# A state-space branch woven into six attention layers: which channels share a group, and how many groups one summing pass takes

## The reference, cut to what matters

```python
def step(hc, inp):                 # state-space branch, per channel d (256) and state n (16)
    a, b = inp
    hc = a * hc + b
    return (hc, hc)
...
A_disc = jnp.exp(delta[..., None] * A)
B_x = delta[..., None] * Bm[:, :, None, :] * x1[..., None]
...
y = jnp.einsum('tbdn,btn->btd', hs, Cm)      # a sum over the 16 states
out = (jax.nn.silu(g) * y) @ out_W + out_b
...
for i in range(DEPTH):             # second branch: six layers, windows of 32 tokens, 16 heads of 64
    x = attn_layer(shift_tokens(x), ...) + x
    x = ffn_layer(shift_tokens(x), ...) + x
...
x + s * silu(x_second)             # s is the first branch's result
```

## Time and profile before

| | us |
|---|---|
| median of three runs | 1931.85 |
| the profiled execution | 1930.3 |
| its span, first to last instruction | 1928.5 |
| TensorE busy in the span | 1756.7 |
| VectorE / GpSimd / ScalarE busy | 1596.1 / 1527.8 / 1252.5 |
| the 16 DMA engines, mean busy share | 32% |

### The profile page before, as it was taken

One profiled execution on the slowest core, in us unless ns is written; L12 is line 12 of the kernel. 1 busy time (PEld: TensorE's weight loads), 2 busy tenths in 40 slices (PEclk: granted clock), 3 DMA queues, 4 the chain that ended last, 5 costly groups with the idle time before them and its releaser, 6 DMA issues. The chain is left out here.

```text
span 1928.5 us, 73996 instructions
## 1 busy us (share of the span) xinstructions
PE 1756.7 (91%) x30944; PEld 999.4 (52%) x30944; DVE 1596.1 (83%) x2736; ACT 1252.5 (65%) x2339; POOL 1527.8 (79%) x1348
## 2 busy tenths in 40 slices
PE   3798999999999999999999999999999999999862
PEld 1355555555555555555555555555555555555420
DVE  5777998888888897889988898889878798888536
ACT  3566676676676676776776676676766666766630
POOL 1765899878998789878998789888888689987640
PEclk9999999999999999999999999999999999999975
DMA  3114234153313334142332433342331534123321
GB/s 109 29 39 70 45 71 79 37 85 49 66 33 67 72 61 71 41 71 55 68 71 37 87 49 59 74 79 39 67 58 33 100 62 63 30 45 58 54 23 44
DMA packets 95607, 113.14 MB, mean 59 GB/s; under 512 B 42334, under 2 KB 61548, under 8 KB 95276
## 3 DMA queue, kind: packets, MB, share of 16 engines
q1 hardware_dynamic: 95276, 108.41, 31.1%
HBM read 19.22 MB, written 1.05 MB: 11 GB/s over the span
## 5 line engine op out<-in xcount | busy, mean ns | idle before, releaser
L1315 POOL TENSOR_TENSOR AB<-qc,qn 128x512 f32<-128x512 f32 x384 | 494.6, 1298 | 21.4 <-DVE qn L1109 21.4
L1326 POOL TENSOR_TENSOR AB<-AB,rinv 128x512 f32<-128x512 f32 x384 | 402.0, 1062 | 24.5 <-DVE rinv L1132 24.5
L559 PE MATMUL bank<-wqkv,XT 128*128 128x512 f32 x768 | 400.2, 614 | 12.2 <-DVE qn L1109 12.2
L1333 POOL TENSOR_TENSOR Pb<-Pb,p_rden 128x512 f32<-128x512 f32 x192 | 200.1, 1042 | 235.2 <-DVE p_rden L1153 234.1
L848 ACT ACTIVATE qkT<-bank 128x512 f32<-128x512 f32 x384 | 229.2, 597 | 209.3 <-PE bank L584 208.6
L1109 DVE TENSOR_TENSOR qc<-bank,rt 128x512 f32<-128x512 f32 x384 | 261.3, 680 | 123.4 <-ACT sq L839 108.9
L584 PEld LDWEIGHTS bank<-ident,AB 128*128 128x128 f32 x1536 | 181.7, 142 | 181.9 <-issue 119.3
L839 ACT ACTIVATE sq<-bank 128x512 f32<-128x512 f32 x384 | 228.1, 594 | 66.4 <-PE bank L559 57.3
L1109 DVE TENSOR_TENSOR qn<-bank,rt 128x512 f32<-128x512 f32 x384 | 261.4, 681 | 0.0
L584 PE MATMUL bank<-ident,AB 128*128 128x128 f32 x1536 | 241.5, 280 | 13.3 <-ACT qkT L848 6.2
L1116 DVE TENSOR_REDUCE ssq<-sq 128x8 f32<-128x512 f32 x384 | 251.2, 670 | 0.0
(11 more groups left out here) (137 smaller groups left out, 2657.3 us busy)
## 6 DMA issues: line engine op xcount, KB each, us to landing
V<-V SPq DMA_DIRECT2D x672, 64.0 KB, 2.1
rep<-du SPq DMA_DIRECT2D x64, 512.0 KB, 7.3
wqkv<-in_Wqkv SPq DMA_DIRECT2D x36, 256.0 KB, 3.7
XV<-XT SPq DMA_DIRECT2D x96, 64.0 KB, 2.8
wo<-in_Wo SPq DMA_DIRECT2D x6, 512.0 KB, 4.1
BC<-BC SPq DMA_DIRECT2D x8, 256.0 KB
w<-in_W SPq DMA_DIRECT2D x6, 341.0 KB, 3.2
BC<-BC SPq DMA_DIRECT2D x8, 128.0 KB
```

What stands on the lines that cost most here:

```text
L559: pe.matmul(R[u % 2][:], XT[:, s % NB, (u % 2) * P:(u % 2 + 1) * P], wqkv[:, (u // 2) * 512:(u // 2 + 1) * 512], start=True, stop=True).th ...
L1315: pool.tensor_tensor(AB[:, n % NAB, :], qc[:, u % 2, :], qn[:, u % 2, :], ALU.add).then_inc(rs_done, 1)
L1326: pool.tensor_tensor(o, o, r, ALU.mult).then_inc(nm_done, 1)
L1333: pool.tensor_tensor(Pb[:, g % 2], Pb[:, g % 2], r, ALU.mult).then_inc(pn_done, 1)
```

## The change

Four things change, and the orders of all engines with them.

1. A transfer of `replicate` takes every eighth channel, `du[r::8]`, where it took 16 neighbours, `du[r:r + 16]`. The amount and the packets are the same. The rows of `A`, the columns of `in_W` and `in_b` that belong to the gate, and the rows of `out_W` are put into the matching order outside of the loop, when the inputs are laid out.
2. `ZSUM` is 4: `z_sum` takes 4 chunks, one for each strip, and there are 4 calls per batch. `chunk` numbers the chunks so that four in a row lie in four transfers and four strips; a transfer's two chunks are j and j + 4.
3. `NH` goes from 5 to 8 (`hb`), `NAB` from 12 to 9 (`AB`).
4. The lists of all engines are in another order, and some operations have another lag: `turn_p(i, 3)` and `value(i + 1, 1)`, `value(i + 1, 2)` end an iteration where they began the next; `norm_x` begins VectorE's odd iterations where it ended the even ones; the `z_` operations are spread over the phases in another way.

The hunks of ScalarE's and VectorE's lists are left out but for a few lines, and GpSimd's is cut to its last part.

```diff
@@ -38,24 +38,24 @@
 
 
 BSTEP = 6
-NAB = 12
+NAB = 9
 NREP = 4
-NH = 5
-ZSUM = 2
+NH = 8
+ZSUM = 4
 ROWS16 = (0, 2, 4, 6, 1, 3, 5, 7)
 BC_IN = 8 * 16
 V_IN = 7 * 16
 FIRST_TO_LAST = range(-2, STEPS + 9)
-T_ORDER = [("turn_p", 3, 1, 1), ("turn", 0, 0, 1), ("turn", 1, 0, 1), ("turn", 2, 0, 1), ("turn", 3, 0, 1),
-           ("turn_p", 0, 0, 1), ("turn", 4, 0, 1), ("turn", 5, 0, 1), ("turn_p", 1, 0, 1), ("turn", 6, 0, 1),
-           ("turn", 7, 0, 1), ("turn_p", 2, 0, 1)]
+T_ORDER = [("turn", 0, 0, 1), ("turn", 1, 0, 1), ("turn", 2, 0, 1), ("turn", 3, 0, 1), ("turn_p", 0, 0, 1),
+           ("turn", 4, 0, 1), ("turn", 5, 0, 1), ("turn_p", 1, 0, 1), ("turn", 6, 0, 1), ("turn", 7, 0, 1),
+           ("turn_p", 2, 0, 1), ("turn_p", 3, 0, 1)]
 X_ORDER = [("values_out", 3, 1, 1), ("scores", 0, 0, 1), ("scores", 1, 0, 1), ("values_out", 0, 0, 1),
            ("scores", 2, 0, 1), ("values_out", 1, 0, 1), ("scores", 3, 0, 1), ("values_out", 2, 0, 1)]
-M_ORDER = [("z_x", 0, -1, 6), ("z_dbc", 0, 1, 6), ("z_out", 0, 9, 6), ("z_g", 0, 5, 6), ("z_dup", 0, 1, 6),
-           ("z_decay", 13, 8, 6), ("z_decay", 1, 4, 6), ("z_decay", 6, 6, 6), ("z_decay", 2, 4, 6),
-           ("z_decay", 7, 6, 6), ("z_decay", 3, 5, 6), ("z_decay", 8, 7, 6), ("z_decay", 14, 8, 6),
-           ("z_decay", 9, 7, 6), ("z_decay", 10, 7, 6), ("z_decay", 4, 5, 6), ("z_decay", 15, 8, 6),
-           ("z_decay", 11, 7, 6), ("z_decay", 12, 7, 6), ("z_decay", 0, 3, 6), ("z_decay", 5, 5, 6)]
+M_ORDER = [("z_dbc", 0, 1, 6), ("z_out", 0, 9, 6), ("z_dup", 0, 1, 6), ("z_x", 0, -2, 6), ("z_g", 0, 4, 6),
+           ("z_decay", 8, 6, 6), ("z_decay", 14, 8, 6), ("z_decay", 9, 6, 6), ("z_decay", 0, 3, 6),
+           ("z_decay", 15, 8, 6), ("z_decay", 5, 5, 6), ("z_decay", 3, 4, 6), ("z_decay", 11, 7, 6),
+           ("z_decay", 1, 3, 6), ("z_decay", 4, 4, 6), ("z_decay", 12, 7, 6), ("z_decay", 10, 6, 6),
+           ("z_decay", 6, 5, 6), ("z_decay", 13, 7, 6), ("z_decay", 7, 5, 6), ("z_decay", 2, 3, 6)]
 
 
 def befores(order):
@@ -374,8 +374,8 @@
 
         def chunk(j):
 
-            n = 2 * (j // 4) + j % 2
-            return n, ROWS16[n], (j // 2) % 2
+            n = 4 * (j // 8) + j % 4
+            return n, ROWS16[n], (j // 4) % 2
 
         def xpair(s):
             b = s % NB
@@ -493,39 +493,39 @@
                 sp.wait_ge(delta_done, b + 1)
                 k = 8 * b + n - NREP
                 if k >= 0:
-                    chunks = 16 * (k // 8) + 4 * (k % 8 // 2) + 3 + k % 2
+                    chunks = 16 * (k // 8) + 8 * (k % 8 // 4) + 5 + k % 4
                     sp.wait_ge(dA_done, chunks)
                     sp.wait_ge(bu_done, chunks)
-                r = 16 * ROWS16[n]
+                r = ROWS16[n]
                 sp.dma_start(rep[:, (8 * b + n) % NREP].rearrange("p z c t -> p (z c t)"),
-                             du[r:r + 16].rearrange("d (o z) c t -> d o (z c t)", o=1).broadcast_to([16, 8, 2 * DBLK * SEQ]))\
+                             du[r::8].rearrange("d (o z) c t -> d o (z c t)", o=1).broadcast_to([16, 8, 2 * DBLK * SEQ]))\
                   .then_inc(rep_in[(8 * b + n) % NREP], 16)
 
             for i in FIRST_TO_LAST:
-                replicate(i - 4, 2)
-                next_qk(i, 1)
-                replicate(i - 7, 5)
                 replicate_bc(i - 3, 0)
-                replicate(i - 6, 4)
-                replicate_bc(i - 4, 4)
-                replicate(i - 3, 0)
+                replicate_bc(i - 3, 1)
+                next_qk(i, 2)
+                spread(i, 0)
                 next_v(i, 0)
+                replicate_bc(i - 3, 2)
+                replicate(i - 5, 4)
+                replicate_bc(i - 3, 3)
+                replicate_bc(i - 3, 4)
+                next_qk(i, 3)
+                replicate(i - 6, 6)
                 arrange_x(i + 2)
-                replicate(i - 7, 6)
-                replicate(i - 7, 7)
-                replicate_bc(i - 3, 1)
-                replicate_bc(i - 3, 2)
-                spread(i, 0)
-                next_qk(i, 2)
-                replicate(i - 5, 3)
-                replicate(i - 3, 1)
                 spread(i, 1)
-                next_qk(i, 3)
+                replicate(i - 5, 5)
+                spread(i, 2)
+                spread(i, 3)
                 next_v(i, 1)
-                spread(i, 2)
+                replicate(i - 6, 7)
                 next_qk(i + 1, 0)
-                replicate_bc(i - 3, 3)
-                spread(i, 3)
+                replicate(i - 3, 2)
+                replicate(i - 3, 3)
+                replicate(i - 2, 0)
+                next_qk(i + 1, 1)
+                replicate(i - 2, 1)
                 other_weights(i)
 
         @block.tensor
@@ -760,64 +760,60 @@
             pe.wait_ge(pool_set, POOL_SET)
             pe.wait_ge(mask_set, 2)
             for i in FIRST_TO_LAST:
-                z_x(i + 1)
-                turn_p(i - 1, 3)
-                value(i, 1)
-                value(i, 2)
+                z_dbc(i - 1)
                 turn(i, 0)
                 values_out(i - 1, 3)
+                turn(i, 1)
                 value(i, 3)
-                turn(i, 1)
-                qk(i + 1, 0)
-                qk(i + 1, 1)
                 scores(i, 0)
                 turn(i, 2)
-                z_sum(i - 5, 0)
+                z_out(i - 9)
+                qk(i + 1, 0)
+                z_dup(i - 1)
+                z_x(i + 2)
                 w_out(i - 2, 0)
-                z_dbc(i - 1)
                 turn(i, 3)
-                z_out(i - 9)
-                z_g(i - 5)
+                qk(i + 1, 1)
+                scores(i, 1)
+                turn_p(i, 0)
                 qk(i + 1, 2)
-                z_dup(i - 1)
-                scores(i, 1)
+                z_g(i - 4)
+                w_gelu(i - 3, 0)
+                turn(i, 4)
+                w_out(i - 2, 1)
+                values_out(i, 0)
                 qk(i + 1, 3)
-                w_out(i - 2, 1)
-                turn_p(i, 0)
-                w_gelu(i - 3, 0)
+                w_gelu(i - 3, 1)
                 qk(i + 1, 4)
-                turn(i, 4)
-                values_out(i, 0)
-                w_gelu(i - 3, 1)
+                w_out(i - 2, 2)
                 turn(i, 5)
+                w_gelu(i - 3, 2)
                 qk(i + 1, 5)
-                w_out(i - 2, 2)
-                w_gelu(i - 3, 2)
                 scores(i, 2)
                 turn_p(i, 1)
+                w_gate(i - 3, 0)
                 qk(i + 1, 6)
-                w_gate(i - 3, 0)
                 w_out(i - 2, 3)
                 turn(i, 6)
                 values_out(i, 1)
-                z_sum(i - 8, 6)
                 w_gate(i - 3, 1)
                 turn(i, 7)
-                z_sum(i - 7, 4)
                 qk(i + 1, 7)
-                z_sum(i - 5, 1)
                 w_gate(i - 3, 2)
-                mean_x(i - 2)
                 scores(i, 3)
                 turn_p(i, 2)
+                mean_x(i - 2)
                 value(i + 1, 0)
-                z_sum(i - 6, 2)
+                w_down(i - 3)
+                z_sum(i - 4, 0)
+                z_sum(i - 7, 2)
+                z_sum(i - 6, 1)
+                z_sum(i - 8, 3)
                 var_x(i - 2)
-                z_sum(i - 6, 3)
-                z_sum(i - 7, 5)
-                w_down(i - 3)
-                z_sum(i - 8, 7)
                 values_out(i, 2)
+                turn_p(i, 3)
+                value(i + 1, 1)
+                value(i + 1, 2)
 
         @block.scalar
         def _(act):
@@ -1019,68 +1015,68 @@
...
+                scale_x(i - 3)
-                scale_x(i - 3)
...
-                z_exp_x(i)
+                z_exp_x(i + 1)
...
-                z_softplus(i - 2)
+                z_softplus(i - 1)
...
+                z_exp_g(i - 4)
-                z_exp_g(i - 5)
...
@@ -1236,58 +1232,58 @@
...
+                norm_x(i - 3)
-                norm_x(i - 2)
...
-                z_conv(i + 2)
-                z_scan(i - 5, 6)
+                z_scan(i - 6, 10)
+                z_scan(i - 7, 13)
 
...
@@ -1402,61 +1398,61 @@
...
                 z_hc(i - 8, 13)
-                z_hc(i - 6, 6)
-                z_hc(i - 4, 1)
-                z_bu(i - 7, 12)
-                z_hc(i - 6, 7)
-                z_hc(i - 5, 3)
-                z_hc(i - 8, 14)
-                normalise(i, 7)
-                rotate_sum(i + 1, 4)
-                rotate_sum(i + 1, 5)
                 z_hc(i - 7, 10)
                 normalise_p(i, 2)
+                z_hc(i - 8, 14)
+                z_bu(i - 5, 9)
+                z_hc(i - 7, 11)
+                z_bu(i - 3, 3)
+                z_hc(i - 8, 15)
+                z_silu_g(i - 4)
+                z_bu(i - 7, 14)
                 z_silu_x(i)
-                z_hc(i - 4, 2)
-                z_silu_g(i - 5)
-                z_hc(i - 8, 15)
-                z_bu(i - 4, 3)
-                z_delta(i - 2)
-                z_bu(i - 4, 4)
```

(126 more changed lines are left out.)

84 lines of the change are left out of this document (27 added, 57 removed).

## The result

The changed kernel takes 1868.19 us (median of four runs, 1866.89 to 1872.40) against 1931.18 us: a ratio of 0.968 with a 95% interval of 0.9651 to 0.9709, 63 us faster. The forecast was 1865 us. The kernel before varies more from run to run than the changed one (1916.80 to 1936.25 us over all its runs beside the experiments), so a difference of a few us between two medians of different experiments is not certain.

A forecast was written before the change was run, and what follows sets the result against it. The prediction took TensorE's list to bound most iterations. Sums 27, transfers 24, orders 10 and drain 4 made 65 us off 1930.3, so 1865 us (chance 0.55), with a range from 1840 to 1901 us.

The forecast's parts named there:

- The cause of "issue": TensorE's mid-call stalls, 36.1 us in 21 places: an instruction fetch waits behind a `replicate` transfer on its DMA engine.
- The transfer's own price: Every eighth channel read in `replicate`: about 2.5 us of DMA engine time instead of 5, landing in 4.5 to 5 us.
- The value of the transfers: TensorE's "issue" waits in the middle fall from 36.1 to 12 us, so 24 us go.
- The slot of four strips: One `z_sum` over four strips on TensorE takes 1.00 us, where one over two strips takes 0.98 us.
- The value of the sums: Fewer `z_sum` slots on TensorE save 3.84 us per batch, in full in seven of eight batches: 27 us.
- The orders: New engine lists: half of the 20.0 us that `turn_p` waits for GpSimd's `normalise_p` goes, 10 us.
- The drain: End of the kernel: eight `hb` buffers and fewer z operations left over save 4 us, between 0 and 8.
- Fetches not helped: Rival 0.13: the transfer is bound at the writing side or by packets and still lands after 7.3 us; 1889 us.
- strips two by two: Rival 0.10: four strips run as two pairs on TensorE, a group takes 1.96 us and the sums gain nothing; 1892 us.
- The fourth: Rival 0.05: evening out one phase fills another, the orders give the gains back, no net change; 1930 us.
- the third: Rival 0.10: all 36.1 us of "issue", all 20.0 of `normalise_p` and 8 in the drain go; 91 us, 1839 us.
- The last one: Rival 0.07: `z_sum` on TensorE waits for GpSimd's products, 3.9 us in each of 28 groups, 109 us lost; 1974 us.

The follow-up runs named there:

- e2: The kernel before with only the new transfer, `replicate` reading every eighth channel, and inputs laid out to match: 1879.66 us, ratio 0.9748.
- e9: The changed kernel with each `replicate` transfer followed by a second of the same rows and amount to device memory that nobody reads: 1882.15 us.
- e3: The changed kernel with each four-strip sum cut in two, two strips in place and two behind the following `values_out(i, 2)`: 1872.92 us.
- e8: The kernel before with transfers of every eighth channel and every second `z_sum` cut to 16 of its 512 columns: 1874.48 us.
- e11: The changed kernel with 4 of 8 products of `w_out` and 2 of 3 of `w_down` run on 16 of 512 columns: 1862.40 us.
- e1_neighbours: The changed kernel with the old transfer, `replicate` reading 16 neighbouring channels again, and the input order with it: 1935.36 us.

## Why the prediction was right or wrong

**The total** is right, 1865 against 1868.19 us, but by luck: two errors of some 25 us each cancel in it.

**The cause of "issue"** is right: stalls in the middle of a call, no semaphore, an instruction packet that mostly starts only behind the transfers, and a product 2.2 to 2.8 us after it, 33 times of 33. `e2` takes the stalls away with the transfer alone, `e9` brings a part back with no later datum.

**The transfer's own price** is right: 2.5 us of engine time and 4.5 to 5 us to land, measured 512 KB at 200 GB/s (2.6 us) and 4.8 us. The Trainium skill's rule of the ports (page "SBUF — State Buffer", Door 1) stood beside it with an estimate of 2.4 us, which agrees.

**The value of the transfers** is wrong. The step that failed: "That is a third of what there was: 12 of 36.1 us stay, **24 us** go." It is 52 us alone, or 67 us in the new order. Two things were missing. Nearly all stalls went: 15 runs of 5 to 6 us remained in the middle, as forecast, but no "issue" was longer than 1.2 us, so blocks of equal length don't cost the same in another place of the list. And a stall can cost more than its gap, when TensorE comes back at half clock. The profile had shown that. The middle's mean clock was 0.99, a hundredth that I passed over, and at 466.8 us the view says 0.50.

**The slot of four strips** is right: 1.00 us forecast, 1.01 measured. The Trainium skill's ratio for three strips (page "TensorE: Matmul & The Clock Gate", Part 3), from which the prediction estimated some 0.1 us more, is not borne out here.

**The value of the sums** is wrong. The step: "What is taken off that list shortens them one for one". The 27 us are 5 (`e3`, `e8`). I read two iterations in which TensorE was never idle or nearly so (35.10 of 35.10 us and 0.9 us of idle) and took "most iterations" from them. In the iterations of that kind the step holds, as phase 2 of `e8` shows. But the calls of `z_sum` lie in phases 0, 1, 2 and 5, and already in the next iteration that I read, phase 1, TensorE had 2.8 us of idle time, so that a slot less there only makes the idle time longer. The other engines are also close behind where it has none: `e11` shows that with more taken off, TensorE waits.

**The orders** were given 10 us by halving the waits for `normalise_p`; those waits rose by 13 us. What the orders and buffers are worth together is the 7 us between `e2` (1879.66) and `e3` (1872.92), and without the new transfer nothing: the change but for the transfer is as fast as the kernel before or 3 to 4 us slower, and its paired transfers make more stalls (47.5 us against 36.1). The forecast of the phases held in the batch shown for phase 1 (36.7 us, forecast 37 to 38) and the others (37.3 at most, forecast 38); over all batches but the first the longest are 38.3 and 37.8 us.

**The drain** was given 4 us of at most 8; the end is 9.4 us shorter (125.8 us against 135.2). The buffers and orders suffice for that (`e1_neighbours` has 125.9), but the new transfer alone brings 5.8 us of it too (`e2` has 129.4); the two don't add.

**The rivals.** Fetches not helped, and strips two by two: both refuted. The fourth, that the orders give the gains back, did not come either. Of the third, its 36 us of "issue" came true and its 20 us of `normalise_p` did not. The last one, a wait for the products of a sum in the middle, doesn't occur: L744 waits once, 5.3 us, in the drain.

## What to carry to other kernels

A matmul group that stops half-way with "issue" is short of instructions in these traces: look at which transfers run then and how much is queued ahead, and whether a half clock follows; the middle changed here by 1.2 times (43 of 36.1 us) and 1.5 times (65 of 44.2 us) the gaps that went. Don't carry a busy share of 100% in one iteration over to all of them: ask in which iterations the work stands that you take off, and how long the engine is idle in just these. Where three engines are each busy for 82 to 92% of the span, taking some hundred us off one engine's list can bring as little (2 to 15 us) as moving one operation (4 to 7 us for one swap).

## What the runs showed of the hardware

A transfer that reads 16 neighbouring SBUF partitions eight times each ran at 103 GB/s and landed after 7.3 us; with every eighth of 128 partitions it ran at 200 GB/s and landed after 4.8 us, with every second of 32 it landed after 4.6 us. While such transfers ran, instruction packets of queue 8 started mostly at their end (35 of 41 in `e1_neighbours`), up to 10.1 us after the first of the pair shown. In 33 of 33 stalls of 1.5 us and more the next product came 2.2 to 2.8 us after such a packet had started. 8 of the 15 stalls of 1.5 to 3.2 us in the kernel before were followed within 6 us by a stretch at a granted clock of 0.50. Four float32 sums into four column strips had a slot of 1.01 us, two had 0.98.
